# A gated state-space layer and a quantised feed-forward on one core: absolute weight sums and silu of z on ScalarE, roundings and scale products on GpSimd, and a new order of all pieces

## What is computed

```
x = x + tanh(g_xattn) * ssm(ctx, z=layernorm(x))
x = x + tanh(g_ffn) * ffn(layernorm(x))

ssm:  x = in_proj(ctx);  u = silu(conv4(x) + conv_b)
      dt, Bm, Cm = x_proj(u);  delta = softplus(dt_proj(dt) + dt_proj_b)
      for t: state = state * exp(delta_t * A) + delta_t * u_t * Bm_t     # 16 states per channel
             y_t = sum_n state * Cm_t
      y = (y + D * u) * silu(z)
ffn:  bitlinear(x, w) = act_quant(x) @ weight_quant(w).T
      act_quant: scale = 128 / max|x| per token; clip(round(x*scale), -128, 127) / scale
      weight_quant: scale = 1 / mean|w|;     clip(round(w*scale), -1, 1) / scale
      inter = silu(gate(x)) * up(x)                      # 1024 wide
      down(fwht(inter))                                  # Walsh-Hadamard transform over 1024
```

## Time and profile before

| | us |
|---|---|
| median of 3 runs | 246.78 |
| lowest and highest | 245.07, 247.25 |
| profiled execution | 242.07 |
| its span | 240.3 |
| busy in it: DVE, PE, ACT, POOL | 209.9, 182.2, 156.9, 145.2 |

### The profile page before, as it was taken

One profiled execution on the slowest core, in us unless ns is written; L12 is line 12 of the kernel. 1 busy time (PEld: TensorE's weight loads), 2 busy tenths in 40 slices (PEclk: granted clock), 3 DMA queues, 4 the chain that ended last, 5 costly groups with the idle time before them and its releaser, 6 DMA issues. The chain is left out here.

```text
span 240.3 us, 3694 instructions
## 1 busy us (share of the span) xinstructions
PE 182.2 (76%) x1209; PEld 150.0 (62%) x1216; DVE 209.9 (87%) x340; ACT 156.9 (65%) x271; POOL 145.2 (60%) x213
## 2 busy tenths in 40 slices
PE   2779649978896499998598859776687886594954
PEld 2537537957785378787397747665575675463853
DVE  3569999999998979799999999999999975489944
ACT  2485995999019998799159998977667306523040
POOL 1100498495997009699999963999950599055300
...
GB/s 65 233 350 194 1 0 4 0 0 3 1 0 3 0 0 0 4 1 0 0 3 0 0 23 3 0 26 0 0 0 4 22 25 0 0 0 0 23 25 44
DMA packets 8149, 6.34 MB, mean 26 GB/s; under 512 B 2202, under 2 KB 7874, under 8 KB 8130
## 3 DMA queue, kind: packets, MB, share of 16 engines
...
## 5 line engine op out<-in xcount | busy, mean ns | idle before, releaser
L1228 POOL TENSOR_SCALAR driveT<-duT,BT 128x256 f32<-128x256 f32 x120 | 61.2, 528 | 25.1 <-ACT duT L941 17.7
L924 ACT ACTIVATE decay<-delta,zero_c,aneg 128x255 f32<-128x255 f32 x128 | 64.7, 589 | 1.9 <-DVE delta L1394 1.6
L1412 DVE TENSOR_TENSOR prod<-state,BC 128x1024 f32<-128x1024 f32 x32 | 38.6, 1205 | 3.2 <-issue 2.7
L463 PE MATMUL PY<-id,prod 128*128 128x128 f32 x256 | 34.2, 280 | 5.3 <-DVE prod L1412 3.2
L1370 DVE TENSOR_TENSOR_SCAN state<-decay,BC 128x512 f32<-128x512 f32 x30 | 36.4, 1212 | 1.0 <-ACT decay L924 0.9
L1370 DVE TENSOR_TENSOR_SCAN state<-decay,UP 128x512 f32<-128x512 f32 x30 | 36.1, 1204 | 1.0 <-issue 0.9
L463 PEld LDWEIGHTS PY<-id,prod 128*128 128x128 f32 x256 | 29.8, 145 | 6.8 <-DVE prod L1412 4.0
L1253 POOL TENSOR_TENSOR wnat<-wnat 128x512 f32<-128x512 f32 x18 | 23.1, 1282 | 16.6 <-DVE wnat L1493 15.8
L407 PE MATMUL UP<-id,driveT 128*128 128x128 f32 x120 | 20.9, 303 | 5.8 <-DVE state L1370 5.8
L407 PE MATMUL BC<-id,driveT 128*128 128x128 f32 x120 | 21.0, 304 | 3.1 <-POOL driveT L1228 1.5
L1254 POOL TENSOR_TENSOR wnat<-wnat 128x512 f32<-128x512 f32 x18 | 22.9, 1270 | 0.0
...
## 6 DMA issues: line engine op xcount, KB each, us to landing
...
```

Of the source, the lines that this page charges most:

```text
L463: last = nc.tensor.matmul(PY[:, E * c + P * h:E * c + P * (h + 1)], prod[:, g % RING, h, n, P * c:P * (c + 1)], id32[:], is_transpose=True ...
L924: last = nc.scalar.activation(decay[:, m % RING, h, n, 1:L], delta[:, b % 2, h, 1:L], ACT.Exp, bias=zero_c[:], scale=aneg[:, h, NB * j + n ...
L1228: last = nc.gpsimd.tensor_scalar(driveT[:, m % RING, c, n], duT[:, b % 2, c], BT[:, b % 2, c, NB * j + n:NB * j + n + 1], 1.0, ALU.mult, A ...
L1412: nc.vector.tensor_tensor(prod[:, g % RING].rearrange("p h n l -> p h (n l)"), state[:, g % STATES].rearrange("p h n l -> p h (n l)"), PC. ...
```

## The change

1. `weight_abs(m)` is an ACT activation (Abs, with the sum over the free axis as second output) instead of a DVE reduction; its place in ACT's queue is ahead of softplus(0), ahead of decays(0) and behind decays(5).
2. `silu_z(n)` reads x itself and takes the normalisation as scale and bias: two 256-wide activations instead of one 512-wide, and no `norm_z` on POOL.
3. For batches 0 to 2 `round_tokens` and for batches 0 and 1 `round_down` are POOL instructions (`round_tokens_early`, `round_down_early`); the later ones stay on DVE.
4. The scale products `gs` and `us` of all four batches are POOL instructions (`token_factors`), with waits for their last readers.
5. `fold_last` is DVE's alone, all 128 columns of each block.
6. The pieces of every queue stand in a new order; the loose code at the start is put into functions for that.

```diff
             def silu_z(n):
-                act.wait_ge(pool_zn, n + 1)
+                act.wait_ge(dve_r1, 1)
                 if n >= 1:
                     act.wait_ge(pe_szT, n)
-                nc.scalar.activation(sz[:], zn[:], ACT.Silu, bias=zero_c[:]).then_inc(act_sz, 1)
+                for h in range(HALF):
+                    i = HALF * n + h
+                    last = nc.scalar.activation(sz[:, h], xs[:, n, h], ACT.Silu, bias=mr1[:, i:i + 1], scale=r1[:, i:i + 1])
+                last.then_inc(act_sz, 1)
...
+            def weight_abs(m):
+                act.wait_ge(ld_w[m], 16)
+                nc.scalar.activation(wq[:, m], wnat[:, m], ACT.Abs, bias=zero_c[:], accum_out=wsum[:, m:m + 1]
+                                     ).then_inc(wabs_done, 1)
...
+            def token_factors(f):
+                pool.wait_ge(dve_amax, f + 1)
+                pool.wait_ge(dve_winv, 1)
+                if f >= 1:
+                    pool.wait_ge(act_sg, LC * f)
+                    pool.wait_ge(dve_mul, LC * f)
+                for c in range(LC):
+                    nc.gpsimd.tensor_scalar(gs[:, c:c + 1], amax[:, c:c + 1], wmean[:, 0:1], 1.0, ALU.mult, ALU.mult)
+                for c in range(LC):
+                    last = nc.gpsimd.tensor_scalar(us[:, c:c + 1], amax[:, c:c + 1], wmean[:, 1:2], 1.0, ALU.mult, ALU.mult)
+                last.then_inc(pool_gs, 1)
...
-            def norm_z(n):
+            def round_tokens_early(f):
+                pool.wait_ge(act_xr, f + 1)
+                nc.gpsimd.tensor_scalar(q[:], xn[:], MAGIC + QB - 1, MAGIC, ALU.min, ALU.subtract).then_inc(rounded, 1)
+
+            def round_down_early(f, t):
+                pool.wait_ge(act_tq, LC * f + t + 1)
+                nc.gpsimd.tensor_scalar(q2[:, t], tq, MAGIC + QB - 1, MAGIC, ALU.min, ALU.subtract).then_inc(rounded_down, 1)
...
-            fold_last(0, pool, nc.gpsimd, slice(DVE_COLS, P), pool_fold_last)
-            fold_last(1, pool, nc.gpsimd, slice(DVE_COLS, P), pool_fold_last)
+            token_factors(3)
...
             def token_scale(f, link):
 
                 dve.wait_ge(act_xn, f + 1)
+                if f >= 1:
+                    dve.wait_ge(pool_gs, f)
                 link(nc.vector.tensor_reduce(amax[:], xn[:], AX.X, ALU.max, apply_absolute_value=True))
...
-                for c in cols:
-                    nc.vector.tensor_scalar(gs[:, c], amax[:, c], wmean[:, 0:1], None, ALU.mult)
-                for c in cols:
-                    ins = nc.vector.tensor_scalar(us[:, c], amax[:, c], wmean[:, 1:2], None, ALU.mult)
-                ins.then_inc(dve_gs, 1)
...
+            def fold_last(t):
...
+                for i in range(FOLDS):
+                    src, dst = ((inter, fold), (fold, inter))[i % 2]
+                    gap = NI >> (i + 1)
+                    src, dst = (v[:, t].rearrange("p (g s w) -> p g s w", s=2, w=gap * P) for v in (src, dst))
+                    nc.vector.tensor_tensor(dst[:, :, 0, :], src[:, :, 0, :], src[:, :, 1, :], ALU.add)
+                    nc.vector.tensor_tensor(dst[:, :, 1, :], src[:, :, 0, :], src[:, :, 1, :], ALU.subtract).then_inc(dve_fold, 1)
```

654 lines of the change are left out of this document (340 added, 314 removed).

## The result

Over twenty runs each, the changed kernel takes 242.61 us (239.80 to 247.58) where the kernel before takes 245.65 (242.14 to 247.25): a ratio of 0.989, with a 95% interval of 0.984 to 0.993. It is faster by 1.1%, where the prediction had 5.1% (234.1 us), and the time lies above its range, which ended at 241.5 us. Ratios leave out executions more than 1.5% above the fastest of their kernel: six of eleven of the kernel before beside the last two runs with short roundings (246.2 to 246.9 us, the other five 242.0 to 244.0), some single ones elsewhere, and one of 405.24 us (weight sums back on DVE) and one of 547.33 us (long roundings where nobody queues). The profiled execution of the changed kernel is the longest of its twenty (247.58 us).

The account below looks back on a forecast made before the run. VectorE was taken as the bound from 26.2 to 195.6 us. Terms +1.4, -3.5, -5.2, -3.4, -2.0 sum to -12.7 on a 240.3 us span: 227.6, with run distances 1.8 and 4.7 kept 234.1 us; range 228.5 to 241.5.

Parts of the forecast that it names:

- the price of a rounding on GpSimd: On POOL, 56.6 to 195.6 us: a token rounding takes 0.75 us and a down rounding 1.2.
- the slower rival: POOL's roundings hold up drives and PE's queue; 2.5 us late at each of seven gives 251.6 us; chance 0.04.
- Its own limit: Delay per POOL rounding at which the change turns from faster to slower: 12.7 / 7 = 1.8 us.
- the tight one: q2_T(1,0) in PE's queue ahead of drive_rows(28,0) and C_rows(26), waiting for POOL's rounding: DVE waits about 0.3 us.
- the layout: Queue schedule laid out by hand with ideal hand-overs; undiscounted it gave -18.0 us, 228.8 us.
- DVE's products waiting for BC with PE waiting for POOL's wq: Trace sign, wq or q, that the prediction is wrong because POOL's roundings hold up the drives.
- Start: +1.4: 0 to first scan: weight sums on ACT delay the first scan from 26.2 to about 27.6 us.
- 26.2 to 56.6 us: -3.5: Two weight sums off DVE -4.4, first_rstd's small instructions moved earlier -0.7, waits for ACT's decays +1.6.
- The rival on ACT: ACT or PE becomes the bound, ACT's busy time 32.2 us in 26.2 to 56.6: 241.0 us; chance 0.17.
- Work off DVE: -5.2: 56.6 to 195.6 us: three token roundings (1.4), four down roundings (2.4) and scale products (1.4) leave DVE for POOL.
- DVE's idle time: -3.4: 56.6 to 195.6 us: half of DVE's 6.8 us of idle time goes.
- The end: -2.0: 195.6 to 240.3 us: earlier PE transposes, whole folds on DVE and scale products give -3.9, half taken.

Follow-up runs that it names:

- short roundings: Changed kernel with its seven GpSimd roundings as multiply and add instead of minimum and subtract, clamp at 127 left out: 230.70 us, 0.938.
- long roundings where nobody queues: Changed kernel with five of seven early roundings back on DVE; tokens of batch 0 and down tile (1,1) stay on GpSimd: 236.36 us, 0.961.
- small parts: Kernel before, in its own order, with silu of z wholly on ScalarE, products gs and us on GpSimd, last folds wholly on DVE: 244.43 us, 0.998.
- first experiment: Changed kernel plus seven forms of a GpSimd operation, each run twice in GpSimd's idle start: 241.19 us, 0.985.
- two short roundings: Changed kernel with only tokens of batch 2 and down tile (1,0) rounded by multiply and add, clamp left out, plus six GpSimd probe forms: 237.54 us, 0.975.
- transposes behind: Changed kernel with q2_T(1,0) put behind drive_rows(28,1) and tokens_T(2) behind drive_rows(29,0) in PE's queue: 238.72 us, 0.970.
- the one with a quarter of the columns: Changed kernel whose seven GpSimd roundings take only a quarter of their columns, the rest left unrounded: 230.96 us, 0.944.
- PE's early order changed: Changed kernel with roundings on DVE, and C_rows(1) to (3) moved ahead of x_dbl, gate, dt_proj and in_proj work on PE: 237.46 us, 0.966.

## Why the prediction was too low, step by step

A table from the traces: the start of the first scan, of times_C(10) and of residual(3) on DVE, what lies between the first and the last of them and behind them, and how long DVE was idle between (from the windows of each trace). No rounding lies ahead of times_C(10), so the last column, from there to the end, compares the five kernels of the new order with one another where they differ; ahead of it their PE, ACT and DVE run the same instructions.

| kernel | first scan | times_C(10) | residual(3) | first scan to residual(3) | of it DVE idle | residual(3) to the end | times_C(10) to the end |
|---|---|---|---|---|---|---|---|
| before | 26.23 | 87.98 | 196.25 | 170.0 | 7.7 | 44.1 | 152.3 |
| small parts on before | 26.35 | 88.50 | 196.94 | 170.6 | 9.6 | 43.6 | 152.0 |
| changed (trace of first experiment) | 27.75 | 88.21 | 199.81 | 172.1 | 19.8 | 38.2 | 149.8 |
| changed, two short roundings | 26.50 | 88.21 | 197.71 | 171.2 | 18.3 | 38.2 | 147.7 |
| changed, transposes behind | 27.55 | 87.99 | 194.79 | 167.2 | 15.2 | 40.7 | 147.5 |
| changed, roundings on DVE | 27.63 | 90.72 | 195.69 | 168.1 | 10.9 | 39.4 | 144.4 |
| changed, short roundings | 27.53 | 88.93 | 188.81 | 161.3 | 9.2 | 39.5 | 139.4 |

*What failed: the price of a rounding on GpSimd.* "On the line between, a token rounding is 0.75 us and a down rounding 1.2": the line was drawn through rows of multiply and add, and the roundings are minimum and subtract. They take 1.92 and 3.63. Seven of them are 20.3 us where the sum had 7.1, 13.2 us more of POOL's queue, and what that costs is the distance between the changed kernel and the same with short roundings, 0.989 to 0.938, 12.4 us by the ratios, 11.9 by the medians and 10.4 from times_C(10) to the end of two traces. The count of columns was interpolated, and rightly enough (multiply and add take 0.62 and 1.04); the operations, which set the time, were taken as equal. No row of before could have told: it has no minimum on POOL.

*And with it the chance of the slower rival.* Its mechanism is what happened: q2_T stands in PE's queue for POOL, with drive_rows and C_rows behind it. Its own limit, 1.8 us a rounding over seven, is 12.7 us. The measured loss of 12.4 is close to it, and the change came out near no change (in the order of the kernel before the same roundings lose 3.9%). It had 0.04, for one place with less than a microsecond of slack. The two large waits are at two of the seven roundings, the tight one and tokens of batch 1, which the layout had not listed as tight; at two to three times the length its slack was not enough. "DVE's products waiting for BC with PE waiting for POOL's wq" was listed as the sign of it, and is what the trace shows.

*Start: +1.4.* The first scan is at 27.5 to 27.8 us in five traces (four of the table's and the one with a quarter of the columns), at 27.21 with PE's early order changed, at 28.28 in the changed kernel's own trace and at 26.50 in the one with two short roundings: 1.3 later than before on average, with single executions up to 1.0 us off. ACT's timeline in the changed kernel's own trace has a weight sum as two records, 2.2 us together as priced:

```profile
17.52 2.00 ACT L959 ACTIVATE wq<-wnat,zero_c 128x2048 bf16<-128x2048 f32 x1
19.43 0.19 ACT L959 ACTIVATION_READ_ACCUMULATOR wq<-wnat,zero_c 128x1 f32 x1
```

The Trainium skill ("ScalarE: Activation LUTs", rules for kernel authors) budgets about 0.3 us and 0.83 ns an element, an estimate of 2.0 us for this activation. The trace agrees with 1.997 for the activation; the record that reads the sum, 0.19 us, comes on top of it.

*26.2 to 56.6 us: -3.5.* With the start's +1.4 the weight sums' net was about -2, and the experiment that puts them back on DVE measures 1.4 us by the ratios and 2.2 by the spans, so the size is about right. The mechanism is not: the 1.9 us of waits were to be for ACT's decays, and DVE is idle for 2.1 to 6.4 us from the first scan to 57 us (2.1 with short roundings, 6.4 with roundings on DVE), most of it behind PE, for C_rows and drive_rows, and more where PE's granted clock was 0.50. ACT comes next: with PE's early order changed two waits for decays appear, 2.0 us in all. The rival on ACT had also counted two weight sums in this stretch (32.2 us), where one of the two had been placed ahead of the first scan; with one it is 30.0, and the trace of the first experiment has ACT busy for 26.5 of the 29.8 us up to 57.5.

*Work off DVE: -5.2 between 56.6 and 195.6.* From the first scan to residual(3) DVE's busy time fell from 162.3 to 152.3 us, 10.0, where the sum had 4.4 + 0.7 + 5.2 = 10.3 for the two stretches together. Right. A scale product on POOL takes 0.27 us, half the 256-wide row as assumed.

*DVE's idle time: -3.4.* Wrong also with short roundings: 9.2 us idle where 7.7 were before. No half of it went; the new order nearly kept the idle time from growing under less work, no more. The stretch was to end at 184 us and DVE to be 95% busy in it; with short roundings it ends at 188.8, and DVE is 94% busy. In the old order the same kind of freeing turned into idle time whole (7.7 to 9.6 in the kernel with the small parts).

*The end: -2.0.* It gave more, 44.1 to 39.5 us or less, as much as the layout had said before I halved it (3.9) and somewhat over. In the old order with the small parts it is 43.6, so the parts themselves give little, and the order and the clock under it give the rest. PE's mean granted clock was 0.81 in the earlier trace rows over the end and 0.84 with the small parts. The new order, with the same instructions, takes 40.7 us at 0.89 (transposes behind), 39.4 to 39.5 at 0.91 to 0.92 and 38.2 at 0.99: 2.5 us for 0.10 of clock. By that slope, an estimate, about half of the 4.6 us is the clock, and the -2.0 of the sum is about what is left for the order. The folds are 3.9 us long with each instruction at 0.68 to 0.69, as priced: the full width on DVE costs nothing more than 352 columns beside POOL.

The two misses, idle time 3.3 us too hopeful and the end 2.6 us too careful, nearly cancel, and that is luck. With it, and with the rounding at its forecast length, the sum comes out: -12.0 us of span (240.3 to 228.3) against -12.7. The traced execution of the kernel before is 3.6 us under the median of its twenty, that of the kernel with short roundings 0.5 under its own; by the ratio the kernel with short roundings gives 6.2%, 15 us.

*What the order is worth* by ratios: small parts 0.998; with the new order but the weight sums still on DVE 0.970; with them on ACT 0.965; with short roundings on POOL 0.938. The step of 2.8% is the order's, and the last of 2.7% (with the clamp left out) is what the roundings' move could have given. Of the 6.8 us between the spans of these two (235.1 and 228.3) 5.0 come from times_C(10) on, 0.6 more than the 4.4 us of DVE work that short roundings free; the other 1.8 lie ahead of it, where the two kernels are the same and PE's granted clock from 38 to 50 us was 0.50 in one and 1.00 in the other. Of the order's 6.8 us the two traces show 3.2, with 4.1 gained at the end; the profiled execution of the small parts is the fastest of its twelve, 2.1 us under their median, which is most of what is missing.
